# A graph network on one core: inverse square roots computed by VectorE alone, and the attention's evacuation copies placed one row later on ScalarE

## The reference

```
h = relu(layernorm(x));  x = x + gat(h)          # attention over the edges, softmax per row, elu
h = relu(layernorm(x));  x = x + gcn(h)          # 3 convolutions, each relu, layernorm, residual
h = relu(layernorm(x));  x = x + gated(h)        # 5 recurrent steps, then two dense layers
h = relu(layernorm(x));  x = x + bilinear(h)     # edge weights, two products, leaky relu
layernorm(x) = (x - mean) / sqrt(var + 1e-5)     # per row of 128
gcn scales rows by 1 / sqrt(degree)
```

## Time and profile before

| quantity | value |
|---|---|
| time before, median of 3 runs | 2556.15 us (2552.11 to 2556.16) |
| the profiled execution | 2560.41 us, span 2558.6 us |
| PE busy | 2258.6 us (88%) |
| DVE busy | 1047.8 us (41%) |
| ACT busy | 941.8 us (37%) |
| POOL busy | 628.7 us (25%) |
| mean granted TensorE clock | 0.929 |

### The profile page before, as it was taken

The page is one execution under the profiler, slowest core; times in us unless marked ns, Lnnn a source line. Parts: engine busy times, 40 slices in busy tenths (PEclk is TensorE's granted clock), DMA queues, the critical chain, the costliest instruction groups (busy, mean ns, idle before and its releaser), DMA issues.

```text
span 2558.6 us, 30865 instructions
## 1 busy us (share of the span) xinstructions
PE 2258.6 (88%) x9795; PEld 1247.5 (49%) x9796; DVE 1047.8 (41%) x2801; ACT 941.8 (37%) x1929; POOL 628.7 (25%) x426
## 2 busy tenths in 40 slices
PE   4777776978787699969899999999999999998998
PEld 3444334855454355534444555456445554454544
DVE  4488886988877344533311221222121221112202
ACT  3588987877777233332211111111111111112300
POOL 1000001510000244323344434443344434420000
PEclk9788986579988899979999999999999999999999
DMA  5477773111111211133322232222222231214583
GB/s 165 141 210 208 218 213 98 0 37 46 44 62 52 45 1 13 35 89 58 82 33 41 41 68 38 44 33 59 56 29 45 41 77 17 33 27 140 224 309 108
DMA packets 186160, 209.74 MB, mean 82 GB/s; under 512 B 102412, under 2 KB 163454, under 8 KB 181979
## 3 DMA queue, kind: packets, MB, share of 16 engines
q1 hardware_dynamic: 116074, 157.51, 20.8%
q0 software_dynamic: 56720, 1.28, 6.6%
q10 hardware_dynamic: 13260, 49.53, 5.4%
HBM read 125.44 MB, written 82.84 MB: 81 GB/s over the span
## 4 chain that ended last, share of the span: by engine, by line
PE 51%; DMA 3%; DVE 1%; issue 0%; ACT 0%; DVEq 0%; ACTq 0%
PE banks L1648 23%; PE banks L1673 20%; PE banks L1770 5%; DMA feat<-hnD 3%; PE banks L1726 1%; PE banks L1634 1%; DMA out_dram<-big 0%; PE banks L1735 0%; PE banks L1788 0%; DVE HN L1947 0%; DVE banks L1942 0%; ACT banks L1833 0%; DVE HN L1944 0%; ACT big L1866 0%; PE banks L1751 0%
## 5 line engine op out<-in xcount | busy, mean ns | idle before, releaser
L808 POOL DMA_INDIRECT WT<-lists x391 | 614.4, 1571 | 867.7 <-DMA WT<-lists 851.7
L1648 PE MATMUL banks<-big,feat 125*128 125x500 f16 (+1 forms) x3150 | 606.2, 353 | 20.3 <-DMA feat<-hnD 15.9
L1648 PEld LDWEIGHTS banks<-big,feat 125*128 125x128 f16 x3150 | 306.3, 97 | 310.4 <-DMA feat<-hnD 16.7
L1673 PE MATMUL banks<-H,U 128*128 128x500 f32 (+1 forms) x756 | 302.3, 541 | 9.9 <-issue 9.9
L1673 PE MATMUL banks<-aT,V 128*128 128x500 f32 (+1 forms) x756 | 296.4, 538 | 3.0 <-DVE HN L1947 3.0
L765 PE MATMUL banks<-wide,ohs 128*125 128x500 f16 x628 | 188.1, 443 | 38.8 <-DVE wide L686 23.8
L1673 PEld LDWEIGHTS banks<-aT,V 128*128 128x128 f32 x756 | 143.1, 190 | 145.0 <-issue 97.2
L1673 PEld LDWEIGHTS banks<-H,U 128*128 128x128 f32 x756 | 142.5, 191 | 139.4 <-issue 101.6
L1935 DVE SCALAR_TENSOR_TENSOR HN<-banks,bh,HN 128x500 f32<-128x500 f32 (+1 forms) x70 | 47.8, 683 | 377.0 <-ACT HN L1831 353.9
L1831 ACT ACTIVATE HN<-banks,bs 128x500 f32<-128x500 f32 (+1 forms) x70 | 44.3, 632 | 380.6 <-PE banks L1673 380.6
L686 DVE TENSOR_SCALAR wide<-pairs,wcol 128x500 f16<-128x500 f16 x628 | 176.5, 348 | 0.0
(11 more groups left out here) (267 smaller groups left out, 2377.0 us busy)
## 6 DMA issues: line engine op xcount, KB each, us to landing
big<-WT ACTq DMA_DIRECT2D x25, 1562.5 KB, 7.8
WT<-zero SPq DMA_DIRECT2D x39, 980.0 KB, 6.9
wide<-keyD SPq DMA_DIRECT2D x80, 320.0 KB, 4.2
hTD<-HN SPq DMA_DIRECT2D x40, 250.0 KB
hnD<-stg SPq DMA_DIRECT2D x32, 250.0 KB
feat<-hnD SPq DMA_DIRECT2D x4, 2000.0 KB
H<-hTD SPq DMA_DIRECT2D x16, 500.0 KB
work<-xhD SPq DMA_DIRECT2D x28, 250.0 KB
```

Source lines behind the costliest of these rows:

```text
L808: nc.gpsimd.indirect_dma_start(out=WT, out_offset=bass.IndirectOffsetOnAxis(ap=lists[:, 0, t - first:t - first + 1], axis=0), in_=lists[:, ...
L1648: last = nc.tensor.matmul(SUMS[s % 2][half][:, 0:wid(ch)], rows_, A[:, j, cols(ch)], start=(j == 0 and part == 0), stop=(j == T - 1 and pa ...
L1673: last = nc.tensor.matmul(PS[bank][:, 0:w], wt_[:, kt, g:g + 128], v[:, kt, 0:w], start=(n == 0), stop=(n == len(terms) - 1))
```

## The change

Two things change. The square root, the reciprocal and the single Newton round are replaced by `root`, ten instructions on VectorE: a start value from the bits of the number (one instruction), and three Newton rounds of three instructions. ScalarE's square roots, and the semaphores for them, go away. And in the attention ScalarE's order changes: in a step it runs `shrink` directly behind the first exponential, the first copy of the new cells stands behind the second exponential, not the first, and one copy may stay over for the next step, where it stands behind `shrink`. At g = 1 none stays over.

```
-def newton(V_, done, y, v, tmp):
-    done(V_.tensor_tensor(tmp, y, y, ALU.mult))
-    done(V_.tensor_tensor(tmp, tmp, v, ALU.mult))
-    done(V_.tensor_scalar(tmp, tmp, -0.5, 1.5, ALU.mult, ALU.add))
-    done(V_.tensor_tensor(y, y, tmp, ALU.mult))
+def root(V_, done, y, v, tmp):
+    done(V_.tensor_scalar(y.bitcast(i32), v.bitcast(i32), -0.5, float(0x5F3759DF), ALU.mult, ALU.add))
+    for _ in range(3):
+        done(V_.scalar_tensor_tensor(tmp, y, -0.5, v, ALU.mult, ALU.mult))
+        done(V_.tensor_tensor(tmp, tmp, y, ALU.mult))
+        done(V_.scalar_tensor_tensor(y, tmp, 1.5, y, ALU.add, ALU.mult))
...
# prepare, ScalarE
-                act.wait_ge(dve_did, VAR)
-                nc.scalar.activation(st[:, 1, :], st[:, 0, :], ACT.Sqrt).then_inc(root_r, 1)
                 act.wait_ge(dve_did, SCALED)
# prepare, VectorE: root and the SCALED signal now stand ahead of dve.wait_ge(edge_c, EG)
...
# attention, ScalarE
-                def deviation(ch):
-                    act.wait_ge(var_r, ch + 2)
-                    nc.scalar.activation(st[:, 1, 0:rows[ch]], st[:, 0, 0:rows[ch]], ACT.Sqrt).then_inc(sd_r, 1)
...
+                late = []
                 for s, (ch, g) in enumerate(steps):
-                    late = cells_of(s - 1) if s else []
                     for q in range(rows[ch]):
                         expo(s, q)
+                        if q == 0 and s and s + 1 < len(steps):
+                            shrink(s + 1)
+                        if q == 1 and s:
+                            late += cells_of(s - 1)
                         if late:
                             evac(late.pop(0))
-                        if q == 0 and s and s + 1 < len(steps):
-                            shrink(s + 1)
-                    for e in late:
-                        evac(e)
+                    while len(late) > (0 if ch and g == 1 else 1):
+                        evac(late.pop(0))
...
# attention, VectorE
                 def center(ch):
                     k = rows[ch]
-                    dve.wait_ge(sd_r, ch + 2)
-                    dn(V_.reciprocal(st[:, 2, 0:k], st[:, 1, 0:k]))
-                    newton(V_, dn, st[:, 2, 0:k], st[:, 0, 0:k], st[:, 1, 0:k])
+                    root(V_, dn, st[:, 2, 0:k], st[:, 0, 0:k], st[:, 1, 0:k])
...
# convolutions, VectorE
-                    dve.wait_ge(sd_r, count(s, second))
-                    dn(V_.reciprocal(inv, sd))
-                    newton(V_, dn, inv, var, sd)
+                    dve.wait_ge(var_r, count(s, second))
+                    root(V_, dn, inv, var, sd)
...
# dense part, VectorE (residual)
-                    V_.tensor_scalar(var, mv[:, 0:k, 1], EPS, None, ALU.add).then_inc(var_r, 1)
-                    dve.wait_ge(root_r, ch + 1)
-                    dn(V_.reciprocal(inv, sd))
-                    newton(V_, dn, inv, var, sd)
+                    dn(V_.tensor_scalar(var, mv[:, 0:k, 1], EPS, None, ALU.add))
+                    root(V_, dn, inv, var, sd)
```

More of the change, by code:

```diff
@@ L569, in _ @@
                 done(last)
-                V_.tensor_scalar(st[:, 0, :], mv[:, :, 1], EPS, None, ALU.add).then_inc(dve_did, 1)
+                done(V_.tensor_scalar(st[:, 0, :], mv[:, :, 1], EPS, None, ALU.add))
+                root(V_, done, st[:, 2, :], st[:, 0, :], st[:, 1, :])
+                V_.scalar_tensor_tensor(st[:, 3, :], mv[:, :, 0], -1.0, st[:, 2, :], ALU.mult, ALU.mult).then_inc(dve_did, 1)
                 dve.wait_ge(edge_c, EG)
@@ L1009, in _ @@
                         smooth(ch - 1)
-                    if ch and g == 5:
-                        deviation(ch - 1)
                     if ch and g == 6:
                         clip(ch - 1)
-                    if s == 3:
-                        act.wait_ge(var_r, 1)
-                        nc.scalar.activation(mx[:, 3, :], col[:, 1, :], ACT.Sqrt).then_inc(sd_r, 1)
-                for e in cells_of(len(steps) - 1):
+                for e in late + cells_of(len(steps) - 1):
                     evac(e)
@@ L1020, in _ @@
                 smooth(SC - 1)
-                deviation(SC - 1)
                 clip(SC - 1)
@@ L1311, in highs @@
                         high(G[(s // SC + 1) % 2], s % SC * NQ + q)
-                def root(s, second):
-                    act.wait_ge(var_r, count(s, second))
-                    nc.scalar.activation(st[:, second, 1, 0:k_of(s)], st[:, second, 0, 0:k_of(s)], ACT.Sqrt).then_inc(sd_r, 1)
                 def norm1(s):
@@ L1358, in _ @@
                     if ch and l == CL - 1:
-                        root(s - 1, 1)
-                    root(s, 0)
-                    if ch and l == CL - 1:
                         norm2(s - 1)
@@ L1367, in _ @@
                         highs(s)
-                root(S - 1, 1)
                 out(S - 3)
```

51 lines of the change are left out of this document (12 added, 39 removed).

## The result

The changed kernel takes 2516.32 us (median of four runs, 2514.72 to 2518.34), against 2556.15 us (2552.11 to 2559.73) for the kernel before, in runs that stood side by side. The ratio is 0.9845, with a 95% interval from 0.983 to 0.9859: some 40 us faster. The profiled execution of the changed kernel took 2518.34 us, with a span of 2516.4 us.

The account below looks back on a forecast made before the run. It took the attention as bound by a loop of waits, VectorE's stream its longest part. From 2560.4 us, attention -37.5, prepare -3.1, convolutions +7.4 and dense +1.5 gave 2528.7, or 2525 us predicted against the median; range 2509 to 2541.

Parts of the forecast that it names:

- The signs asked for: Attention: exponential waits under 20 us, window some 38 us shorter; prepare: `affine` 3 us earlier; borders: aT waits near 3 us.
- Roots in the attention: Attention: six roots on VectorE's path -8.9 us, the degrees' root -1.4, the seventh chunk's root +0.75.
- The copies' order: Attention: moving the first copy behind the second exponential gives back 28 us of 40 us of waits; bounds nothing and all 40.
- The second deduction: Attention: TensorE's clock still falls after `shape` and `center`; 1 us left for each of six chunks.
- Prepare: Prepare: `affine` no longer waits for the table load and starts earlier, -3.1 us.
- Convolutions: Convolutions: five extra instructions cost +1.0 us at each border, more in the last layer and tail; +7.4 us, bounds 4 and 11.
- Dense part: Dense part: two roots of +0.75 us on the chain to the sweep, +1.5 us; the earlier ones have slack.
- Rival 2: Attention: TensorE's clock stays up and all 40 us of wait come back, 12 us better, 2513 us; chance 0.17.
- Rival 1: Attention: TensorE's turns and products become the loop, only 14 us come back, 2539 us; chance 0.2.
- Rivals 3 and 4: Attention: the new order does nothing, 2552 us, chance 0.05; the left-over copy starves TensorE, 2572 us, chance 0.03.
- rival 5: Whole kernel: roots paid everywhere, convolutions +28 us, and the order gives little; 2563 us at 10 us back; chance 0.03.

Follow-up runs that it names:

- fillers: Changed kernel plus TensorE products whose result nobody reads, six at g = 3 and eleven at g = 4 in the attention: 2516.69 us, ratio 0.9828.

## Why the prediction held, point by point

From profile to profile the kernel is 2560.4 - 2518.3 = 42.1 us faster, and the sum had 31.7. Of the 10.4 us between them 7.7 lie in the attention, 1.9 in `prepare` and 3.0 in the counts, which the change does not touch; the sweep, the gated steps and the convolutions are together 2.1 us longer than in the sum. The signs asked for are there: no table load in the attention behind the first exponential, VectorE's wait for exponentials at 0.8 us, `affine` 2.5 us earlier, waits for aT of 3.05 and 3.02 us at the borders and of 0.84, 0.41 and 0.88 us in the last layer.

**Roots in the attention** (forecast -8.9 - 1.4 + 0.75 = -9.55). Given the new order, the roots bring 382.1 - 371.6 = 10.5 us: 8.4 in the six steps with `center` (47.3 and 38.9 us together), 1.5 in the step with the degrees' root (8.2 and 6.7). Taken alone they bring 14.7, with 10.3 us in the six steps, 1.1 in the degrees' and 2.5 in the five steps behind them at g = 6. Why the six steps give 1.9 us more in the old order stays open. The price of the chain stood as I had worked it out. VectorE in `center` of chunk 0, changed kernel:

```profile
585.74 0.17 DVE L155 TENSOR_SCALAR sta<-sta 125x4 int32<-125x4 int32 x1
585.93 0.16 DVE L157 SCALAR_TENSOR_TENSOR sta<-sta 125x4 f32<-125x4 f32 x1
...
587.51 0.16 DVE L159 SCALAR_TENSOR_TENSOR sta<-sta 125x4 f32<-125x4 f32 x1
587.71 1.11 DVE L1113 TENSOR_SCALAR work<-work,mv,sta 125x128 f32<-125x128 f32 x4
```

Ten instructions in 587.71 - 585.74 = 1.97 us. The instruction on the bits, which no row of before had shown, takes 0.17 us like its neighbours; so the upper end of 0.1 us more a root fell away. The Trainium skill (ScalarE: Activation LUTs, What ACT_TABLE_LOAD costs) states a drain of 1.38 us at each switch of tables; by an estimate from that figure the six roots would have given 6 x 2.8 = 17 us more than forecast. The roots alone brought 14.7 us in all and not 26, so this case's runs do not show it.

**The copies' order** (forecast -28, the largest term, and the one that was off). It brought 34.7 us alone, and 402.1 - 371.6 = 30.5 on top of the roots. With both halves the attention is 45.2 us shorter, where the sum had 37.5: 7.7 us are missing from it. The mechanism was right, as the wait of 44.8 us and its fall to 4.5 in the kernel with the order alone show. The step that was mis-sized is the deduction "In the sixteen four by four steps its 5.36 us stand against VectorE's 5.0: 16 x 0.36 = 5.8 us stay". The 5.36 us run from the first turn to the end of the last product. But the next turn starts before that product has ended, so what counts is the spacing from start to start, and that is 5.10 us where one step follows another without a gap. From the changed kernel's timeline of TensorE:

```profile
652.76 1.04 PE L1029 MATMUL banks<-ident,z 125*125 125x125 f32 x8
653.63 1.01 PE L1009 MATMUL banks<-work 125*128 125x500 f32 x2
654.47 1.03 PE L1029 MATMUL banks<-ident,z 125*125 125x125 f32 x8
655.34 2.68 PE L1009 MATMUL banks<-work 125*128 125x500 f32 x6
657.86 0.38 PE L1029 MATMUL banks<-ident,z 125*125 125x125 f32 x2
```

TensorE is no faster in the new order. The same work in the kernel before, where TensorE comes from another product and not from a gap, starts at the same distances:

```profile
587.73 1.04 PE L1061 MATMUL banks<-ident,z 125*125 125x125 f32 x8
588.61 1.01 PE L1041 MATMUL banks<-work 125*128 125x500 f32 x2
589.45 1.03 PE L1061 MATMUL banks<-ident,z 125*125 125x125 f32 x8
590.32 2.68 PE L1041 MATMUL banks<-work 125*128 125x500 f32 x6
```

The steps of four by four cells take 5.00 us each (at g = 0 and g = 2 of chunks 1 and 2), four times VectorE's 1.25 of the earlier trace rows. The steps at g = 1 and g = 3 take 5.64 and 5.55, as VectorE has `share` and `scale` to do, and there TensorE catches up the 0.1 us. So nothing of the 5.8 us stayed, and with it the forecast is 28 + 5.8 = 33.8 against 34.7 and 30.5 measured, 43.3 against 45.2 for the whole attention. The second deduction, 6 us for the half clock, was about right, but not because the clock falls behind every `center`. It does behind that of chunk 0, and does not behind that of chunk 1, after a gap of the same length:

```profile
582.74 1.14 PE L1029 MATMUL banks<-ident,z 125*125 125x125 f32 x8 [1.52 <-DVE z L1072]
...
589.86 2.04 PE L1029 MATMUL banks<-ident,z 125*125 125x125 f32 x8 [2.79 <-DVE z L1072]
...
631.68 1.14 PE L1029 MATMUL banks<-ident,z 125*125 125x125 f32 x8 [2.80 <-DVE z L1072]
```

Idle for 2.79 us in place of 3.67, TensorE came back at half clock in the first case, and VectorE then waits 1.76 us for it (at 594.53). With fillers the five steps at g = 6 take 19.7 us in all; in the three profiles with this attention they take 25.4, 23.1 and 24.4. So the half clock costs 3 to 6 us here, 5.7 in the profile of the changed kernel, and the fillers show that it is the cause.

**Prepare** (forecast -3.1). Four profiles with the old root there have 98.7 to 100.4 us, nine with the new one 94.6 to 96.9: on the mean 3.8 us less. In the changed kernel `affine` starts at 63.53, 0.41 us behind the copy ahead of it and 2.5 us earlier than the earlier trace rows. The rest fits the clock: in 67 to 74 us TensorE ran at a granted clock of 0.51 before and of 1.00 after. That this gave the rest is argued from those two windows, not tried.

**Convolutions** (forecast +7.4, measured +7.6, and 10 us of the median come back when they are undone). That the sum fits the profile is luck: its parts are off in both directions, and the clock at the borders hides some of the cost.

At the two borders TensorE's wait for aT rose from 2.06 and 2.05 us to 3.05 and 3.02, the +1.0 each of the forecast. The `outer` ahead of each border now comes 0.4 us late too, which I had not counted. But from the border to the next `outer` it takes 12.0 us where it took 13.0, since TensorE ran there at a granted clock of 0.87 before and of 1.00 after. The timeline of TensorE behind the first border, kernel before:

```profile
943.29 9.03 PE L1282 MATMUL banks<-big,feat 125*128 125x500 f16 x34
```

the kernel with the convolutions as before, whose code there is the same:

```profile
888.27 0.48 PE L1234 MATMUL banks<-cWs,aT 128*125 128x128 f32 x2 [2.07 <-ACT aT L1326]
888.59 7.35 PE L1255 MATMUL banks<-big,feat 125*128 125x500 f16 x34
```

and the changed kernel:

```profile
890.94 0.48 PE L1225 MATMUL banks<-cWs,aT 128*125 128x128 f32 x2 [3.05 <-ACT aT L1313]
891.26 6.93 PE L1246 MATMUL banks<-big,feat 125*128 125x500 f16 x32
...
898.70 0.59 PE L1246 MATMUL banks<-big,feat 125*128 125x500 f16 x2 [0.51 <-DVE feat L1336]
```

So the clock there changes from one execution to another: of eight profiles with the old root in the convolutions, three have 11.3 us between these two `outer`s and five 13.0, all behind a wait of 2.04 to 2.07 us. At full clock in both kernels a border would cost 0.7 us more than before and not 1.0 less, because TensorE then waits 0.51 us for VectorE, whose work for the next layer stands behind the longer root. The mean over the eight profiles with the old root and the three with ten instructions gives 277.2 and 286.0 us, +8.8; that and the 10 us of the median are the better figures.

The last layer's loop cost more: the five intervals shown above grew from 11.9, 12.4, 12.4, 12.5 and 12.2 us to 12.9, 13.0, 13.5, 13.5 and 14.0, 5.4 us in all, where I had 2.7 + 1.0. The step that was too small is "The loop becomes 13.0 us, above TensorE's: +1.0 and then three times 0.6". The 12.0 us behind it were read at the third chunk of the layer. From the fourth on ScalarE copies a result (hs) between `norm1` and aT, which the loop of 12.0 does not contain. In the changed kernel:

```profile
1031.99 0.55 ACT L1299 COPY hs<-banks 128x500 f32<-128x500 f32 x1
```

The copy of aT starts 0.46 us behind its start, at 1032.45. With it the loop is 13.5 us. The last interval grew by 1.8 and not 1.0, since behind the wait of 3.38 us (2.40 before) TensorE ran `outer` at half clock, 1.97 us for 1.14. That only the first of two roots in a row is exposed was right at ten instructions, with 0.16 us to spare. The tail, from the last `outer` to the first product of the gated steps, went from 1124.72 - 1107.81 = 16.9 to 1079.06 - 1060.52 = 18.5 us: +1.6 against +1.75.

**Dense part** (forecast +1.5). The stage is 1.5 us longer in the profiles, and TensorE's last two waits for a turn grew, from 0.73 us to 1.82 and from 1.88 to 3.00:

```profile
2354.85 0.86 PE L1706 MATMUL banks<-ident,big 125*128 125x125 f32 x3 [3.00 <-ACT big L1822]
```

The sweep behind it is 1.1 us longer too, which I had not counted; with the old roots restored it is back at 160.0 us.

**The rivals.** Rival 2 (the whole wait goes, the clock stays up) was half true: the wait went, the clock stayed up behind some gaps only. Rival 1 showed as the 9.8 us of VectorE's waits for TensorE, which are 3.2 us with fillers; it did not become the loop. Rivals 3 and 4 are ruled out by the runs with the order alone and with no copy over, rival 5 by the attention, where the roots gain. The Trainium skill (Perfetto Trace Analysis, Identifying the Most-Contended Engine) asks to optimise the engine with the highest occupancy first. Read as "give it less work" it was not borne out in the attention: with the roots alone VectorE got more work, and the stage became 14.7 us shorter, because VectorE's waits went.

## What to carry to other kernels

When three engines are each busy for three quarters of a stage, look in the in-order queue of each for an instruction that waits for the second engine while the third waits for what stands behind it; moving it one place down was worth 31 to 35 us here and took no added instruction. Before work is moved from a station's round trip to a chain on the receiving engine, ask at each place whether the round trip is exposed: the same edit gained 10 us in the attention and lost 8 to 10 in the convolutions, where a chain one round shorter cost 1.7 us of the last layer in place of 5.3. When two engines are compared as rivals for a loop, take both from start to start of a repetition: from the first start to the last end one reads too much (5.36 us for 5.10). And read the loop at a repetition that holds everything that the steady state holds; here one copy that joins from the fourth chunk on made it 0.5 us longer. A single profile whose stage agrees with a sum does not confirm the parts.

## What the runs showed that I had not expected

- The price of a chain of small dependent instructions on VectorE is very even, 0.20 us from start to start (125x4), in a profile and by the difference of rounds (0.60 us for three), though each is busy for only 0.16 us.
- Where such a chain is covered, its price has a threshold. The second root of a pair in the last layer cost nothing with three rounds (0.16 us to spare) and made ScalarE wait 0.32 us with four, so the fourth round cost 1.0 us a chunk where the third cost 0.6.
- TensorE's granted clock behind a gap is not given by the gap alone. In the changed kernel's profile it came back at half clock after 2.79 us idle (eight transposes in 2.04 us) and at full clock after 2.80 (1.14 us). At the first layer border of the convolutions, with the same code and a wait of 2.04 to 2.07 us, the next interval took 11.3 us in three profiles and 13.0 in five; behind a wait of 3.05 us it took 12.0, behind 3.70 (four rounds) 13.0. What decides it stays open.
- Keeping TensorE at full clock by fillers made the attention 4 to 6 us shorter, and the kernel no faster that four runs could tell from the changed one.
